# Short passages between the layers of a Fourier tokenizer, and in the block behind it: roots at the slots' end, keys in other banks, rows added in pairs on GpSimd

## The chip, the core and the metric

One NeuronCore of a Trainium2 chip runs the whole program. The metric is device microseconds of one execution. The engines are named as in the profile: PE is the matrix engine (TensorE), PEld its weight loads, DVE the VectorE, ACT the ScalarE, POOL the GpSimd and SP the engine whose queue issues the DMAs.

## The reference, cut to what matters

```
# tokenizer, 128 images of 64 x 64 x 3
h = layer_norm(x @ fc0_w + fc0_b)
for i in range(4):
    x1 = irfft2(einsum(rfft2(h)[12 x 12 modes, both corners], w1/w2[i]))   # the "mix" over modes
    x2 = einsum('bchw,oc->bohw', h, conv_w[i]) + conv_b[i]                 # 1x1 convolution
    h  = layer_norm(x1 + x2, ln_g[i], ln_b[i]);  h = gelu(h) if i < 3 else h
h = gelu(gelu(h @ fc1) @ fc2) @ fc3
h = concat(cls_tok, h)                       # 128 x 65 tokens of 64
# scan sublayer, on layernorm(h) = x and its flip xf
h_t = exp(delta A) h_(t-1) + delta Bf x + delta_b Bb xf;   y_t = sum over 16 states of C_n h_n
h = h + (y + x D_skip + xf D_skip) @ W_out.T
# attention and experts, on layernorm(h) = x
x = x + attention(rmsnorm(x));  out = sum over the top 2 of 8 experts of gate * (silu(f w1) * (f w3)) w2
h = h + x + out
```

## The kernel before, in words

**Tokenizer, to 5766 us.** A first pass goes over the 128 images two at a time, and stores each image's activations (1 MB for a pair, `act_scratch`) and its spectrum (`spectrum_in`). Then four layers follow. Each has a mix over the 12 vertical frequencies ky (`pe_mix`, `dve_mix`, `act_mix`: x_in of one ky is loaded and turned, multiplied by that ky's mixing matrix `w_mix`, and stored to `spectrum_out`), and a pass over all images (convolution product from `act_in`, L508, inverse transforms from `z_in`, L495, layer norm, gelu, and the forward transforms for the next layer). The mixing matrix of a ky is made from raw weights: load w_raw, DVE centres it (L1041, L1044), PE spreads it by four products (`pe_combine`, L978) and DVE copies four banks into `w_mix` (L1055).

A **passage** is what lies between such phases. Into the mix, the SP queue (`layer_body` and `sp_layer`) issues the two raw weights, the convolution's weight and bias, four pairs of gain and shift columns, the two rows of gain and shift, and only then x_in of the first two ky. DVE (`dve_layer`) waits for all of `layer_in` before it touches the convolution's weight and then the first raw weight. Out of the mix, `sp_load` issues act_in, z_in, act_in, z_in, and the first instruction of PE needs act_in.

**Block, from 5766.7 us.** 16 groups of 8 images (260 columns of tokens, 128 partitions) go through a software pipeline: in one window w, group w+1 is in its scan, group w in its attention, group w-1 in its experts. A window is a head and then 27 slots, whose order is written out in code for each engine by tables (`DRIVE_AT`, `SCAN_AT`, `READ_AT`, `OUT_AT`, `MEAN_AT`, ...): in slot n, PE does the three products of expert part n (`expert_slot`: w1 L1705, w3 L1710, w2 L1718) and a piece of the attention and the scan; DVE forms the gated hidden rows (L2165) and, a chunk of four states at a time, the scan's inputs (L2091, L2095, L2099), the scan (L2107) and the read product (L2113), whose rows PE multiplies by the output weights (L1741: four matmuls a chunk, one for each state). At the slots' end come the means and squares of three norms, at the next head their inverse roots: ACT guesses them by logs and exps (L1921, L1925), DVE does a Newton step (L2062, L2066, L2070), then xn, its flip xf, ue and un. PE waits there for xf (L1822). The head also holds the router's softmax and top 2 on DVE (L2184 to L2212), whose result PE turns (L1847) and casts to the expert rows (L1691), and the rotary products of queries and keys. The keys' two products (L1842, L1843) use the banks 5 and 6 that the queries' had, and so wait for DVE's L2080. GpSimd does four additions and products of 128 x 260 a window (L2295, L2298).

A dependency reads `wait(e, name, group, count)` in the code; ISA rows in an order listing are the semaphore instructions that stand apart from the work.

## Time and profile before

| | us |
|---|---|
| median of 3 runs | 7341.99 (7340.01 to 7343.35) |
| the profiled execution | 7339.24 |
| its span | 7337.5 |
| PE busy | 6634.3 (90%) |
| DVE busy | 4609.9 (63%) |
| ACT busy | 4417.8 (60%) |
| POOL busy | 3735.1 (51%) |

The program has two parts with different limits. The tokenizer lasts to 5766.7 us, with passages at 776.9, 1848.6, 2920 and 3993 us, where PE has nothing to do. The block lasts from there to the end. Its steady windows repeat every 92.16 us: `blk_bc`, the first work of ACT in a window, starts at 6008.8, and then twelve times every 92.16 us to 7114.8. A profile of the whole mixes them, so the rows below are of single stretches.

How to read it: a timeline row is start, duration, engine, line, operation, output and input, count, and in brackets the idle time of that engine just before it and what released it. Rows with a count join neighbours.

### The profile page before, as it was taken

How to read it: one execution, taken by the hardware profiler on the slowest of the kernel's cores; microseconds unless marked ns; L12 is line 12 of the kernel's file. 1: busy time of each engine (PE TensorE's matmuls, PEld its weight loads, DVE VectorE, ACT ScalarE, POOL GpSimd, SP SyncE). 2: the span in 40 equal slices, each digit the busy share in tenths (PEclk: the TensorE clock that was granted, in tenths of full speed). 3: DMA queues.
4: the chain of work that ended last, by engine and by line, in shares of the span. 5: the costliest groups of instructions: out<-in, count | busy, mean ns of one | idle time of the engine just before them, and what ended most of it. 6: DMA issues, size and time to landing. Idle time of an engine off the chain costs nothing. (4 is left out here: it accounts for less than half of the span.)

```text
span 7337.5 us, 138677 instructions
## 1 busy us (share of the span) xinstructions
PE 6634.3 (90%) x43890; PEld 4056.0 (55%) x43890; DVE 4609.9 (63%) x7185; ACT 4417.8 (60%) x8385; POOL 3735.1 (51%) x1348
## 2 busy tenths in 40 slices
PE   8999799999799998899998899999999578888888
PEld 3444566666566665666665544444444255555555
DVE  8999477777477776577776333333333477777774
ACT  5666466766466766466765577777777434444443
POOL 8999278777178776277775244444444100000000
PEclk9999899999899999999999999999999788888888
DMA  2333455554455554555554311111111333333330
GB/s 98 112 110 113 168 164 165 166 170 158 167 169 165 167 169 150 175 169 165 166 170 146 126 47 53 48 47 47 54 47 47 104 81 74 74 74 74 74 74 3
DMA packets 597030, 835.12 MB, mean 114 GB/s; under 512 B 451944, under 2 KB 493032, under 8 KB 531304
## 3 DMA queue, kind: packets, MB, share of 16 engines
q1 hardware_dynamic: 596968, 834.34, 36.6%
q8 instruction: 33, 0.54, 0.0%
q14 instruction: 29, 0.24, 0.0%
HBM read 477.60 MB, written 356.58 MB: 114 GB/s over the span
## 5 line engine op out<-in xcount | busy, mean ns | idle before, releaser
L949 POOL TENSOR_TENSOR sb_rstd<-sb_var,sb_minus_half 128x16 f32<-128x16 f32 x1280 | 3689.7, 2899 | 2047.8 <-DVE sb_var L900 1019.6
L691 DVE TENSOR_TENSOR sb_unit<-H,sb_rstd 128x512 f32<-128x512 f32 x768 | 529.1, 689 | 684.0 <-POOL sb_rstd L949 545.9
L508 PE MATMUL H<-sb_conv_block,sb_act_in 128*128 128x128 f32 x6144 | 825.3, 283 | 35.4 <-DMA sb_act_in<-act_scratch 28.7
L508 PEld LDWEIGHTS H<-sb_conv_block,sb_act_in 128*128 128x128 f32 x6144 | 731.6, 192 | 150.1 <-issue 140.9
L613 ACT ACTIVATE sb_act_px<-sb_unit 128x512 f32<-128x512 f32 x768 | 484.0, 630 | 499.5 <-DVE sb_unit L697 499.5
L2295 POOL TENSOR_TENSOR blk_pos<-blk_pos,blk_mag 128x260 f32<-128x260 f32 x32 | 22.8, 734 | 1337.3 <-ACT blk_mag L1961 1337.3
L636 ACT ACTIVATE sb_act_out<-TC 128x512 f32<-128x512 f32 x768 | 447.7, 583 | 180.8 <-PE TC L523 180.8
L912 DVE COPY sb_act_out<-TC 128x512 f32<-128x512 f32 x256 | 177.0, 691 | 595.3 <-PE TC L758 595.3
L775 PE MATMUL M<-sb_dense,sb_fc_w 128*64 128x512 f32 x2048 | 521.7, 609 | 30.4 <-ACT sb_dense L858 25.4
L697 DVE TENSOR_TENSOR sb_unit<-sb_unit,sb_shift_row 128x512 f32<-128x512 f32 x768 | 531.4, 692 | 26.1
L694 DVE TENSOR_TENSOR sb_unit<-sb_unit,sb_gain_row 128x512 f32<-128x512 f32 x768 | 531.2, 692 | 26.2
L684 DVE TENSOR_REDUCE sb_var<-sb_square 128x16 f32<-128x528 f32 x768 | 501.1, 694 | 69.7 <-ACT sb_square L606 69.7
L523 PE MATMUL TC<-sb_table,sb_act_px 128*128 128x128 f32 x3072 | 485.0, 281 | 62.5 <-ACT sb_act_out L636 62.1
L858 ACT ACTIVATE sb_dense<-M,sb_fc_shifted 128x512 f32<-128x512 f32 x512 | 323.8, 683 | 291.3 <-PE H L767 291.3
L537 PE MATMUL TP<-sb_act_px,sb_table 128*52 128x256 f32 x3072 | 496.5, 402 | 0.0
L523 PEld LDWEIGHTS TC<-sb_table,sb_act_px 128*128 128x128 f32 x3072 | 333.4, 142 | 256.0 <-ACT sb_act_px L613 218.6
L606 ACT ACTIVATE sb_square<-H 128x512 f32<-128x512 f32 x768 | 417.0, 600 | 94.7 <-PE H L516 94.7
L2009 ACT ACTIVATE blk_silu<-bank 114x260 f32<-114x260 f32 x384 | 148.6, 387 | 524.0 <-PE bank L1710 523.8
L516 PE MATMUL H<-sb_v_sb,sb_table 52*128 52x512 f32 x1536 | 433.7, 641 | 0.0
L495 PEld LDWEIGHTS M<-sb_table,sb_z_in 96*52 96x52 f32 x6144 | 357.5, 128 | 113.3 <-issue 81.8
L495 PE MATMUL M<-sb_table,sb_z_in 96*52 96x128 f32 x6144 | 404.6, 274 | 0.0
L864 ACT ACTIVATE sb_dense<-M,sb_fc_bias 128x512 f32<-128x512 f32 x512 | 352.0, 688 | 85.0 <-PE M L775 60.2
(274 smaller groups left out, 12749.6 us busy)
## 6 DMA issues: line engine op xcount, KB each, us to landing
act_scratch<-sb_act_out SPq DMA_DIRECT2D x256, 1024.0 KB, 3.9
sb_act_in<-act_scratch SPq DMA_DIRECT2D x256, 1024.0 KB, 5.3
spectrum_in<-sb_f_sb SPq DMA_DIRECT2D x512, 78.0 KB, 1.8
sb_x_in<-spectrum_in SPq DMA_DIRECT2D x48, 832.0 KB, 4.4
spectrum_out<-sb_y_sb SPq DMA_DIRECT2D x48, 832.0 KB, 4.6
sb_z_in<-spectrum_out SPq DMA_DIRECT2D x512, 78.0 KB, 5.1
blk_rows_b<-scan_rows SPq DMA_DIRECT2D x128, 260.0 KB, 6.6
blk_rows_bb<-scan_rows SPq DMA_DIRECT2D x128, 260.0 KB, 7.5
```

Of the source, the lines that this page charges most:

```text
L495: mm = e.matmul(M[u][64 * t:64 * t + 52, 128 * g:128 * g + 128], z, gb[:, t], start=True, stop=True, skip_group_check=True)
L508: e.matmul(H[j][:, 128 * u:128 * u + 128], act_in[p][:, 128 * b:128 * b + 128], conv_block[:, :], start=(u == 0), stop=False, skip_group_c ...
L523: mm = e.transpose(TC[:, 128 * u:128 * u + 128], act_px[k % 2][:, 128 * u:128 * u + 128], const("ident"))
L537: mm = e.matmul(dst, const("f1"), src[:, :, 16 * h:16 * h + 16], start=True, stop=True, skip_group_check=True)
L613: e.activation(act_px[k % 2][:, :], unit[k % 2][:, :], gelu).then_inc(px_ready, 1)
L636: e.activation(act_out[q][:, 512 * k:512 * k + 512], TC[:, :], ACT.Copy).then_inc(act_ready, 1)
L684: e.tensor_reduce(var[j][:, :], square[j % 2][:, :].rearrange("p (y c) -> p y c", c=C + 1), AX.X, ALU.add).then_inc(var_ready, 1)
L691: e.tensor_tensor(rows, H[k][:, :].rearrange("p (y c) -> p y c", c=C), rstd[k][:, :].unsqueeze(2).to_broadcast([128, 16, C]), ALU.mult).th ...
L694: e.tensor_tensor(rows, rows, gain_row[:, :].unsqueeze(1).to_broadcast([128, 16, C]), ALU.mult).then_inc(scaled, 1)
L697: e.tensor_tensor(rows, rows, shift_row[:, :].unsqueeze(1).to_broadcast([128, 16, C]), ALU.add).then_inc(affine_ready, 1)
L775: mm = e.matmul(FC1[w][64 * v:64 * v + 64, :], fc2_w[:, :], dense1[2 * w + v][:, :], start=True, stop=True, skip_group_check=True)
L949: e.tensor_tensor(rstd[j][:, :], var[j][:, :], minus_half[:, :], ALU.pow).then_inc(rstd_ready, 1)
```

## The change

Tokenizer. The gain and shift columns, which the last layer alone reads, are loaded once at the start. The convolution's weight and bias and the first two raw weights of a layer are loaded during the phase before (`sp_conv`), with a semaphore of their own (`conv_in`). In the passage SP issues x_in first, then the two rows, then both act_in (`sp_load_act`), which before were issued after the mix. DVE centres ky 0 and PE does its convolution product and first combine in banks of H, ahead of the waits for the last activations and spectra. After the mix, only z_in is left to load. At the start, the queue has four more DMAs ahead of the first image.

Block. The guesses, the table load and the Newton steps of the scan's and the experts' norm move from the next head to the slots' end. The keys' products go to banks 1 and 2, and wait for `bc` and `soft_pos` (ACT's reads of these banks) instead of `rope` 2. The first cast of the gate moves behind the first w1 product. GpSimd adds xn and xf into xs, so that the skip takes one product instead of two, and for each chunk adds the second half of its rows to the first (128 x 520), so that the output takes two matmuls instead of four.

The SP queue from the end of the first pass. In the listing `sb_` tiles are the tokenizer's, and act_scratch, spectrum_in and spectrum_out are in HBM. Before:

```order
L1190 DMA sb_w_raw<-in_w_mix_dram 128x416
L1192 ISA
L1062 ISA
L1062 DMA sb_conv_raw<-in_conv_w_dram 32x32
L1063 ISA
L1063 DMA sb_bias_raw<-in_conv_b_dram 32x1
L1068 REGISTER_ALU
L1072 DMA sb_gain<-in_ln_g_dram 32x1
L1073 DMA sb_shift<-in_ln_b_dram 32x1
```

and after:

```order
L1216 ISA
L972 DMA sb_x_in<-spectrum_in 128x1664 x2
L1205 REGISTER_ALU
L1075 ISA
L1075 DMA sb_gain_row<-in_ln_g_dram 128x32
L1076 DMA sb_shift_row<-in_ln_b_dram 128x32
L1208 REGISTER_ALU
L234 ISA
L258 DMA sb_act_in<-act_scratch 128x2048 x2
L1192 UNCONDITIONAL_BRANCH
L1192 ISA
L970 ISA
```

The loads of x_in have moved ahead of all, and the two of act_in stand where the mix's own loads of w_raw (L970) come next.

PE at the head of a window, from the keys' products (`blk_wk_rot`) to the second slot. `blk_lg` holds the gate, `blk_gate_t` the gate turned, `blk_ue` and `blk_ug` are the experts' inputs. Before:

```order
L1843 MATMUL bank<-blk_un,blk_wk_rot 128x260
L1569 ISA
L1847 MATMUL bank<-blk_tables,blk_lg 16x65 x4
L1691 MATMUL bank<-blk_gate_t,blk_pick 128x260
L1569 ISA
L1700 MATMUL bank<-blk_res,blk_tables 128x260
L1705 MATMUL bank<-blk_ue,blk_experts 114x260
L1569 ISA
L1710 MATMUL bank<-blk_ug,blk_experts 114x260
```

and after:

```order
L1862 MATMUL bank<-blk_un,blk_wk_rot 128x260
L1582 ISA
L1866 MATMUL bank<-blk_tables,blk_lg 16x65 x4
L1713 MATMUL bank<-blk_res,blk_tables 128x260
L1718 MATMUL bank<-blk_ue,blk_experts 114x260
L1704 MATMUL bank<-blk_gate_t,blk_pick 128x260
L1582 ISA x2
L1727 MATMUL bank<-blk_ug,blk_experts 114x260
```

The cast (`blk_pick`) has moved behind the residual's product and the first w1 product.

ACT at the slots' end, where `blk_sn` is the scan's norm, `blk_mn` the experts' and `blk_an`, `blk_un` the attention's. Before:

```order
L2011 ACT_TABLE_LOAD
L1569 REGISTER_ALU
L1886 ACTIVATE blk_sn_sqr<-bank 128x260
L1887 ACTIVATE blk_h_cen<-bank 128x260
L1892 ACTIVATE blk_mn_sqr<-blk_x 128x260
L1903 ACTIVATE blk_h<-bank 128x260
L1897 ACTIVATE blk_an_sqr<-bank 128x260
L1898 ACTIVATE blk_cen<-bank 128x260
L1609 REGISTER_ALU
L1609 COMPARE_AND_BRANCH
L1921 ACTIVATE blk_sn_log<-bank,blk_tables 128x260
```

and after:

```order
L1904 ACTIVATE blk_sn_sqr<-bank 128x260
L1905 ACTIVATE blk_h_cen<-bank 128x260
L1582 REGISTER_ALU
L2031 ACTIVATE blk_silu<-bank 114x260
L1910 ACTIVATE blk_mn_sqr<-blk_x 128x260
L2046 ACT_TABLE_LOAD
L1921 ACTIVATE blk_h<-bank 128x260
L1932 ACTIVATE blk_sn_log<-bank,blk_tables 128x260
L1932 ACTIVATE blk_mn_log<-bank,blk_tables 128x260
L1582 ISA
L1936 ACTIVATE blk_sn_y<-blk_sn_log 128x260
```

The scan's squares now stand ahead of the last silu, and the two logs ahead of the loop's branch, with the attention's squares behind them.

The diff, cut to its core (in its second half PE's code comes first, then ACT's `guesses`, DVE's `roots` behind the slots, and GpSimd's additions):

```diff
         def sp_load_act(e, P, p, n):
             at_least(e, h_ready, 8 * P + 4 * p - 4)
             e.dma_start(act_in[p][:, :], act_d[n]).then_inc(ld[p], 16)
...
         def pe_combine(e, m, p, layer):
+            banks = H if isinstance(m, int) and q == 0 else COMBINED
...
         def pe_mix(e, m, p, layer, more):
+            if zero:
+                e.wait_ge(w_mix_s, 4 * q0 + 4)
             turn(0)
...
+        def sp_rows(e, norm):
+            g, b = norm
             e.dma_start(gain_row[:, :], g.partition_broadcast(128)).then_inc(layer_in, 16)
             e.dma_start(shift_row[:, :], b.partition_broadcast(128)).then_inc(layer_in, 16)
+        def sp_conv(e, layer):
+            e.dma_start(conv_raw[:, :], io["conv_w"][layer]).then_inc(conv_in, 16)
+            e.dma_start(bias_raw[:, :], io["conv_b"][layer].unsqueeze(1)).then_inc(conv_in, 16)
+            for p in range(2):
+                e.dma_start(w_raw[p][:, :], io["w_mix"][layer, p]).then_inc(w_in[p], 16)
...
             def layer_body(layer, last):
                 for p in range(2):
-                    e.dma_start(w_raw[p][:, :], io["w_mix"][layer, p]).then_inc(w_in[p], 16)
+                    e.wait_ge(st_x[p], 32 * halves * (layer + 1))
+                for p in range(2):
+                    sp_mix_load(e, 0, p, layer)
                 e.wait_ge(act_ready, 8 * halves * (layer + 1))
-                sp_layer(e, layer + 1, layer, (io["ln_g"][layer], io["ln_b"][layer]))
+                sp_rows(e, (io["ln_g"][layer], io["ln_b"][layer]))
+                for p in range(2):
+                    e.wait_ge(st_a[p], 16 * halves * (layer + 1))
+                    sp_load_act(e, halves * (layer + 1), p, p)
                 mix(layer)
...
-        WO_AT, X2_AT, H1_AT = 22, 23, 25
+        WO_AT, X2_AT, H1_AT = 22, 23, 24
-        SKIP_AT = 9
+        SKIP_AT = 12
-        MEAN_AT, VARIANCE_AT = 23, 24
+        MEAN_AT, VARIANCE_AT = 22, 24
...
                     e.matmul(B[0][0:2 * HP, 0:TOK], expert("w1", x, k, 2 * HP), ue[:, :], start=True, stop=True)
+                    if n == 0:
+                        gate_cast(g, 0)
                     if k == 0:
                         wait(e, "ug", g, x + 1)
+                    if n < 2 and attn is not None:
+                        wait(e, "rope", attn, 5 + n)
...
-                    e.matmul(B[7][:, 0:TOK], wskip[:, :], xn[:, :], start=True, stop=False, skip_group_check=True)
-                    e.matmul(B[7][:, 0:TOK], wskip[:, :], xf[:, :], start=False, stop=False, skip_group_check=True)
+                    wait(e, "both", g)
+                    e.matmul(B[7][:, 0:TOK], wskip[:, :], xs[:, :], start=True, stop=False, skip_group_check=True)
...
-                    wait(e, "read", g, k + 1)
-                    for n in range(NC):
-                        mm = e.matmul(B[7][:, 0:TOK], wt("wout"), wide(rows_c, k)[:, TOK * n:TOK * n + TOK],
+                    wait(e, "paired", g, k + 1)
+                    for half in range(2):
+                        mm = e.matmul(B[7][:, 0:TOK], wt("wout"), wide(rows_c, k)[:, TOK * half:TOK * half + TOK],
...
-                    wait(e, "rope", ga, 2)
-                    e.matmul(B[5][:, 0:TOK], wt("wk_t"), un[:, :], start=True, stop=True)
-                    e.matmul(B[6][:, 0:TOK], wk_rot[:, :], un[:, :], start=True, stop=True).then_inc(sig["qk"], 1)
+                    if scan:
+                        wait(e, "bc", gs)
+                        wait(e, "soft_pos", gs)
+                    e.matmul(B[1][:, 0:TOK], wt("wk_t"), un[:, :], start=True, stop=True)
+                    e.matmul(B[2][:, 0:TOK], wk_rot[:, :], un[:, :], start=True, stop=True).then_inc(sig["qk"], 1)
...
+                    if n == VARIANCE_AT:
+                        guesses(w + 1, scan1, moe1)
...
+                roots(w + 1, scan1, moe1)
...
+                    e.tensor_tensor(xs[:, :], xn[:, :], xf[:, :], ALU.add).then_inc(sig["both"], 1)
+                if scan:
+                    for k in range(CHUNKS):
+                        wait(e, "read", gs, k + 1)
+                        rows = wide(rows_c, k)
+                        e.tensor_tensor(rows[:, 0:2 * TOK], rows[:, 0:2 * TOK], rows[:, 2 * TOK:4 * TOK],
+                                        ALU.add).then_inc(sig["paired"], 1)
```

## Rows read from the trace of the kernel before

**Rows 1.** Windows: stretch, its length, busy us (x instructions), PEclk, DMA share, GB/s

```profile
776.90:788.30 11.40, 0.00 (x0) 0.00 (x0) 0.00 (x1) 0.00 (x0) 0.00 (x0) 0.50 0.34 83
895.20:904.60 9.40, 0.00 (x0) 0.00 (x0) 0.00 (x0) 0.41 (x2) 0.00 (x0) 0.68 0.72 229
6009.00:7115.00 1106.00, 922.04 (x3843) 641.75 (x3842) 797.78 (x1392) 473.47 (x1105) 33.74 (x48) 0.87 0.32 74
```

**Rows 2.** Page, DMA issues: count, KB each, us to landing

```profile
sb_act_in<-act_scratch SPq DMA_DIRECT2D x256, 1024.0 KB, 5.3
sb_x_in<-spectrum_in SPq DMA_DIRECT2D x48, 832.0 KB, 4.4
sb_z_in<-spectrum_out SPq DMA_DIRECT2D x512, 78.0 KB, 5.1
```

**Rows 3.** Timeline of SP, first passage into the mix

```profile
776.87 0.78 SPq L264 DMA_DIRECT2D spectrum_in<-sb_f_sb  x2
...
785.21 0.90 SPq L963 DMA_DIRECT2D sb_x_in<-spectrum_in  x2
```

**Rows 4.** Timeline of DVE, first passage and the start of the mix

```profile
788.30 0.21 DVE L1079 COPY sb_conv_rep<-sb_conv_raw 32x128 f32<-32x128 f32 x1 [18.96 <-DMA sb_shift_row<-in_ln_b_dram]
...
797.44 0.56 DVE L1041 TENSOR_REDUCE sb_w_sum<-sb_w_raw 128x13 f32<-128x416 f32 x1
...
801.69 0.86 DVE L1055 COPY sb_w_mix<-TC 128x416 f32<-128x416 f32 x1 [3.06 <-PE TC L978]
```

**Rows 5.** Timeline of PE, start of the mix

```profile
796.51 1.08 PE L992 MATMUL H<-sb_table,sb_x_in 128*128 128x128 f32 x8
...
806.33 1.13 PE L1005 MATMUL H<-sb_w_mix,sb_x_t 128*128 128x128 f32 x8 [0.44 <-ACT sb_x_t L1023]
```

**Rows 6.** Timeline of SP, passage out of the mix

```profile
899.21 0.35 SPq L252 DMA_DIRECT2D sb_act_in<-act_scratch  x1
```

**Rows 7.** Timeline of PE, passage out of the mix

```profile
904.62 2.07 PE L508 MATMUL H<-sb_conv_block,sb_act_in 128*128 128x128 f32 x8 [9.54 <-DMA sb_act_in<-act_scratch]
906.62 3.01 PE L495 MATMUL M<-sb_table,sb_z_in 96*52 96x128 f32 x32
```

**Rows 8.** Timeline of PE, start of the program

```profile
18.82 0.64 PE L294 MATMUL M<-sb_table,sb_image_in 128*96 128x128 f32 x2 [7.53 <-DMA sb_image_in<-in_x_dram]
```

**Rows 9.** Timeline of PE, end of the window 6469.7 to 6561.9

```profile
6545.67 1.92 PE L1741 MATMUL bank<-blk_rows_c,blk_weights 128*128 128x260 f32 x8
...
6558.87 1.21 PE L1822 MATMUL bank<-blk_xn,blk_w_delta 128*128 128x260 f32 x2 [3.46 <-DVE blk_xf L2247]
```

**Rows 10.** Timeline of ACT, end of that window

```profile
6549.34 1.28 ACT L2011 ACT_TABLE_LOAD   x1
...
6554.47 0.48 ACT L1921 ACTIVATE blk_sn_log<-bank,blk_tables 128x260 f32<-128x260 f32 x1
```

**Rows 11.** Timeline of PE, head of that window

```profile
6476.89 1.23 PE L1842 MATMUL bank<-blk_un,blk_weights 128*128 128x260 f32 x2 [3.12 <-DVE blk_tmp L2080]
...
6479.95 0.60 PE L1847 MATMUL bank<-blk_tables,blk_lg 65*16 65x65 f32 x4 [0.96 <-DVE blk_lg L2212]
6481.95 1.23 PE L1691 MATMUL bank<-blk_gate_t,blk_pick 16*128 16x260 f32 x2 [1.40 <-ACT blk_gate_t L1984]
...
6485.01 1.08 PE L1710 MATMUL bank<-blk_ug,blk_experts 128*114 128x260 f32 x2
```

**Rows 12.** Timeline of DVE, that window

```profile
6474.78 0.66 DVE L2196 TENSOR_TENSOR blk_lg<-blk_lg,blk_tables 65x64 f32<-65x64 f32 x1
...
6477.97 0.22 DVE L2196 TENSOR_TENSOR blk_lg<-blk_lg,blk_tables 65x64 f32<-65x64 f32 x1
...
6520.68 1.23 DVE L2113 TENSOR_TENSOR blk_rows_c<-blk_rows_c,blk_rows_b 128x1040 f32<-128x1040 f32 x1
...
6542.77 0.43 DVE L2165 TENSOR_TENSOR blk_hid<-blk_silu,bank 114x260 f32<-114x260 f32 x1 [3.42 <-ACT blk_silu L2009]
```

**Rows 13.** Timeline of GpSimd, that window

```profile
6474.62 0.73 POOL L2298 TENSOR_TENSOR blk_dub<-blk_pos,blk_xf 128x260 f32<-128x260 f32 x1
```

More of the change, by code:

```diff
@@ L1050, in dve_mix @@
             q, q0 = 2 * m + p, NY * layer
+            banks = H if isinstance(m, int) and q == 0 else COMBINED
             since(e, y_pe, 4 * q0, 4 * (q - 1))
@@ L1938, in window, with before @@
                     guess(moe_n, "x")
+            def before(w, scan, attn, moe):
+                scan_square(w, scan)
+                guesses(w, scan, moe)
+            def window(w, scan, attn, moe, scan1, attn1, moe1):
+                gs, ga, gx = w + 1, w, w - 1
+                old = moe and not (isinstance(gx, int) and gx == 0)
                 if attn:
```

112 lines of the change are left out of this document (55 added, 57 removed).

## The prediction, as it was made before the changed kernel had run

> **What bounds the kernel now.** I read the windows view first, to find stretches in which PE has nothing to do, since the page has it at 90% of the span and nothing else near that. Then the timelines of SP, DVE and PE in one such stretch of each kind, then one steady window of the block on every engine.
>
> There are two kinds of stretch. The first are passages between the tokenizer's phases. Before a mix, PE, DVE and ACT all stand still for 11.4 us [rows 1], and the next row of DVE says for what: it sat 18.96 us until the row of shifts had landed [rows 4]. That load is the last of fourteen, most of them tiny, which SP issues between the last spectrum's store at 776.87 and x_in at 785.21 [rows 3]. PE's first turn of x_in comes at 796.51 [rows 5]. After a mix, PE waits 9.54 us for act_in, issued at 899.21, and takes up z_in at 906.62 [rows 6, 7]. All this happens four times.
>
> The second kind are waits inside the block's window. Over twelve windows in 1106 us (92.16 each) PE is busy 922.04, that is 76.8 of 92.2 us [rows 1]. The rest is in two places of a window. At its end PE waits 3.46 us for xf, the last link of squares, logs, roots [rows 9]. In its head it waits 3.12 for the queries' rotation, 0.96 for the gate and 1.40 for the turned gate [rows 11]. DVE is nearly full in the middle, and its first long idle time, 3.42 us, comes at 6542.77, where it waits for ACT behind PE [rows 12]. So from there to the end PE sets the pace, and in the middle both do.
>
> **The passages, part by part.** *Into the mix.* SP's gain and weight loads go out of the way. x_in can go when the stores from 776.87 are in, which I put at 779.4; before it went at 785.21 [rows 3], so it lands 5.8 earlier, and no longer waits for a turn behind the combine: with 4.4 us to land [rows 2] and 1.2 for what it shares with its twin, the first turn is near 785.0 instead of 796.51, 11.5 us earlier. The convolution, centring and combine of ky 0, which filled 788.3 to 796.5, now run before 777, under the last images' work of ACT and SP.
>
> That gain is not kept in full. What is late next is the raw weight of ky 2. It stands behind x_in (2 x 832 KB) and act_in (2 x 1024 KB), 3.7 MB, which at the 229 GB/s of the loads in the other passage [rows 1] take 16.2 us: it lands at 795.6 instead of before 797.44. DVE's centring of ky 2 comes ahead of its copies for ky 1 in its order, and takes 1.2; the copies then begin at 796.8 where they began at 801.69 [rows 4], and the mix of ky 1, which began 4.6 later at 806.33 [rows 5], is 4.9 us earlier. If the weight's packets pass beside the large loads, it is up to 9. I take 6 a layer. Bounds: 2 (x_in slowed by act_in from its own first packet) and 11.5.
>
> *Out of the mix.* act_in is in memory, and L508 (2.07 us) starts at once. z_in goes at 899.21 instead of 0.4 to 3 us behind it, and its landing no longer shares the rings with 2 MB. PE took z_in at 906.62; the second z load now goes at about 899.9, and with between 2 and 5.1 us to land [rows 2] PE takes it at 902 to 905. I take 902.3, so 4.3 less; bounds 1.5 and 4.9.
>
> *At the start* four more DMAs stand before the first image, and PE waits for the image [rows 8]. Fourteen took the 7.6 us between the first row's end and the last row of [rows 3], 0.54 each: +2.
>
> Tokenizer: 4 x (6 + 4.3) - 2 = 39 us less; with all bounds at one side 12 to 64.
>
> **The block, part by part, per window.** *Roots at the slots' end.* ACT's silu of the last part ends as its table load starts, at 6549.34, and the first log is at 6554.47 [rows 10], 5.13 later, because four squares and copies, two means and a third square stand between. Now the scan's squares are before the last silu, and between are one square, the load (1.28) and h, the two at 0.3 each: 1.9. From the log to L1822 the links are the same ones, 4.40 (6554.47 to 6558.87 [rows 9, 10]). So L1822 comes 3.2 us sooner after the last silu. Late next are the attention's squares, which stand behind the guesses. Their roots end at about 2.5 us after xf, and PE has three products and the router's (3.6 us) to do in that time, so this is covered; if not, it costs up to 1. Bounds 2.2 and 3.5.
>
> *Fewer products.* The output takes 8 instead of 16, the skip 1 instead of 2. An L1741 group of four is 1.92 as x8 rows, which is 0.44 for each product, so 9 x 0.44 = 4.0 of PE. It counts only where PE sets the pace: the last two groups (the fourth is that of 6545.67 [rows 9]) and the skip, 5 x 0.44 = 2.2. Bounds 1.3 and 4.0.
>
> *The gate's first cast.* PE waits 1.40 for the turned gate and then does L1691, L1700 and L1705, and w3 at 6485.01 [rows 11]. Now L1700 and L1705, 1.9 together at this clock, run in the wait, and w3 can come when the cast (6481.95 to 6483.1) and ug (0.4) are done, at 6483.8: 1.2 less. Bounds 0 and 1.3. The new wait of slots 0 and 1 for the keys' rotation is met by then: DVE does it right behind the gate's chain, while PE turns the gate.
>
> *The keys' banks.* The 3.12 us wait goes, but the gate's chain on DVE is not shortened by it, and L1847 stays at 6479.95 [rows 11]. The wait is moved, not removed: 0. A price is possible: PE, idle in one piece of 4.5 us instead of 3.1 and 1.0, is at its lower clock for longer. A pair of passes takes about 1.0 us at this clock, against 0.44 after it; four more such products would cost 2.2. Bounds 0 and +2.2.
>
> *GpSimd's additions.* One product of 128 x 260 took 0.73 [rows 13], so one of 128 x 520 is estimated at 1.46, and four and xs are 6.6 us a window. GpSimd has the time, but DVE does not run freely beside it: the same L2196 took 0.66 while GpSimd worked (6474.62 to 6475.35), and 0.22 without [rows 12, 13]. An addition starts when its read product ends, the first at 6521.9 [rows 12], and the fourth falls in DVE's idle time. Three times 1.46 are 4.4 us which DVE can lose, and it had 3.42 of idle time at 6542.77. But PE waits within the middle for hidden rows too, so the idle time at the end does not absorb it all. I take half, +2.2, and +0.2 for xs beside the gate's chain. Bounds 0 and +6.6.
>
> The Trainium skill, SBUF — State Buffer, section "Who interferes with whom", says that a VectorE instruction with two SBUF inputs and a GpSimd instruction that reads SBUF exclude one another for their whole length, whichever came first. The stretched L2196 agrees. By this rule the scan of 2.3 us can also hold back an addition, which would then come to PE 3.8 us after its read; by a rule of shared bandwidth neither would. It is a mechanism of the slower rival, below, and its price there is from the rows.
>
> Sum: -3.2 - 2.2 - 1.2 + 0 + 2.4 = -4.2 us a window. There are thirteen full windows (twelve of the row, and the one before them, of 91.7): -55. The windows that fill and drain the pipeline have the roots or the products, not both: -1 each for four, -4. Block: -59. Bounds with all at one side are -8.8 and +3.9 a window. I hold -7.5 to +0 as its likely part, -100 to 0.
>
> **Total.** 39 + 59 = 98 us less than the profiled execution's 7339.2, 7241. The median of the three runs is 2.8 above that execution, so 7244 as a median.
>
> **Rivals.**
>
> *Only the passages pay.* The additions take back from DVE what PE gains, and a window stays within 1 us of 92.16. For it speaks that DVE is full in the middle and loses up to 4.4; against it, that the roots' 3.2 us lie outside that stretch. Then 7342 - 39 = 7303.
>
> *The block pays in full.* The additions fall beside DVE's work with one input from PSUM, and all nine products count: -8 a window, 13 x 8 = 104. For it speaks that L2165 and L2161 read a bank; against it, that the scan, the three inputs and the read itself have both inputs in SBUF. Then 7342 - 39 - 104 = 7199.
>
> *x_in gains nothing*, because the two act_in share its rings, as they did with z_in, whose median of 5.1 for 78 KB is that of a megabyte. The passages then pay 2 + 4.3 a layer, less 2: 23, and the time is 7342 - 23 - 59 = 7260.
>
> *Slower.* The additions stand in the scan's way, or it in theirs: DVE loses all 6.6 us, and PE, in its order, waits for `paired` about 1 us at the two chunks where product follows read by 3 us (8.6). DVE's lag carries to the last silu, so the roots give nothing; products and cast give 3.4. A window is then 5.2 us longer, 13 windows 68, and 7342 - 39 + 68 = 7371. It decides from 39 / 13 = 3.0 us a window on.
>
> **How the numbers follow.** Forecast 0.50, only the passages 0.15, the block in full 0.18, x_in gains nothing 0.12, slower 0.05. The range for 8 in 10: from the full case, 7195, to the case of the passages alone, 7303. A measurement of this kernel can tell about 0.2%, 15 us, from no change. All cases but the last lie beyond it; some of the case of the passages alone lies within if both bounds are bad. Faster 0.92, same 0.03, slower 0.05.
>
> **What would show it.** In the profile after: DVE's wait for the shift row gone, the first turn about 8 us after the last spectrum store, and then DVE waiting for w_raw of ky 2 in a row of its own; if it does not wait, the passage gives near 11. PE's wait for act_in after the mix replaced by one of some 5 us for z_in. In a steady window, an interval near 88 us, L1822 some 6.7 us after the last silu; L1842 without a wait and L1847 with one of 4 to 5 us; L2107 or L2091 of 1.5 us more than 2.3 and 1.2 where an addition runs beside them; GpSimd's additions of 1.4 to 1.5 us. The forecast is wrong if the window is over 91 or under 85, or if the passages give under 5 us a layer in all.

## The result, and the profile after

| | before | changed |
|---|---|---|
| median us | 7340.75 (5 runs) | 7304.17 (7299.74 to 7311.40, 5 runs) |
| ratio, 95% interval | | 0.995 (0.9936 to 0.9965) |
| span of the profiled execution | 7337.5 | 7297.9 |
| first `blk_bc` of the block | 5784.4 | 5752.4 |
| from there to the end | 1553.0 | 1545.5 |
| mean of twelve steady windows | 92.17 | 91.61 |

Every median is of fast executions; one slow one of experiment 7 (10486.97 us at a granted clock of 0.555) is left out, with which its median would be the 7210 that the expectation of experiment 14 names.

The kernel became 36.6 us faster, where 98 were forecast, and its time is one microsecond above the range. Of the 39.5 us of the span, 32.0 come ahead of the block. The block was to give 59 and gave 7.5 in this execution; the first experiment below has it at nothing.

**The passages.** First SP at the first passage, as [rows 3]; columns as there.

```profile
778.88 0.79 SPq L273 DMA_DIRECT2D spectrum_in<-sb_f_sb  x2
781.23 0.84 SPq L972 DMA_DIRECT2D sb_x_in<-spectrum_in  x2
...
783.61 0.86 SPq L258 DMA_DIRECT2D sb_act_in<-act_scratch  x2
784.99 0.34 SPq L970 DMA_DIRECT2D sb_w_raw<-in_w_mix_dram  x1
```

x_in leaves 2.3 us behind the last store, not 8.3 [rows 3]. Then PE and DVE, which answer to [rows 4, 5]:

```profile
786.43 1.20 PE L1002 MATMUL H<-sb_table,sb_x_in 128*128 128x128 f32 x8 [0.95 <-DVE sb_w_mix L1068]
```

```profile
795.38 0.59 DVE L1053 TENSOR_REDUCE sb_w_sum<-sb_w_raw 128x13 f32<-128x416 f32 x1 [9.01 <-DMA sb_w_raw<-in_w_mix_dram]
796.00 0.59 DVE L1056 SCALAR_TENSOR_TENSOR sb_w_cen<-sb_w_sum,sb_w_raw 128x416 f32<-128x416 f32 x1
796.51 0.85 DVE L1068 COPY sb_w_mix<-TC 128x416 f32<-128x416 f32 x1
```

The first turn is at 786.43 instead of 796.51, and DVE waits 9.01 us for the raw weight of ky 2, up to 795.38 (the prediction had it land at 795.6). Its copies for ky 1 begin at 796.51, 5.2 us earlier than before. Behind the mix and at the start, as [rows 7, 8]:

```profile
901.19 3.66 PE L504 MATMUL M<-sb_table,sb_z_in 96*52 96x128 f32 x32 [6.35 <-DMA sb_z_in<-spectrum_out]
```

```profile
20.80 0.63 PE L303 MATMUL M<-sb_table,sb_image_in 128*96 128x128 f32 x2 [10.32 <-DMA sb_image_in<-in_x_dram]
```

z_in is taken up 5.4 us earlier, and the image 2.0 later. Of the 5.4 us, 2.1 come from ahead of this passage: the mix's last row of PE (L1005, now L1017) starts at 891.57 instead of 893.64. The passage out of the mix alone gives 3.4.

**The block.** The windows view over the twelve steady windows, as the last of [rows 1], and then three stretches of the head of the window from 6436.69 (columns: PE, PEld, DVE, ACT, POOL busy; PEclk, DMA share, GB/s):

```profile
5979.73:7079.09 1099.36, 898.71 (x3626) 602.38 (x3626) 823.22 (x1392) 472.47 (x1104) 158.60 (x108) 0.85 0.31 74
6436.69:6445.69 9.00, 3.67 (x27) 3.02 (x26) 6.04 (x20) 8.99 (x25) 3.50 (x5) 0.88 0.61 160
6445.69:6452.69 7.00, 4.96 (x13) 2.65 (x14) 2.83 (x10) 5.78 (x14) 0.00 (x0) 0.50 1.04 259
6452.69:6458.69 6.00, 6.00 (x16) 3.33 (x16) 2.04 (x5) 1.04 (x3) 0.00 (x0) 0.62 1.04 255
```

and the same three of before (window from 6469.69):

```profile
6469.69:6478.69 9.00, 5.88 (x27) 4.64 (x26) 6.05 (x20) 8.58 (x23) 2.81 (x4) 0.69 0.66 157
6478.69:6485.69 7.00, 4.65 (x13) 2.58 (x12) 2.65 (x10) 6.21 (x14) 0.00 (x0) 0.50 1.05 244
6485.69:6491.69 6.00, 5.92 (x22) 3.38 (x22) 3.23 (x7) 1.35 (x4) 0.00 (x0) 0.96 1.05 232
```

Before, the granted clock was 0.69 in the first nine microseconds and back at 0.96 from 16 us on. Now it is 0.88 in the first nine, where PE mostly waits, and 0.62 from 16 to 22 us, where it works without a pause: 16 instructions in 6 us instead of 22. GpSimd's rows at the end of the middle, then PE and DVE beside them:

```profile
6398.53 6.25 POOL L2337 TENSOR_TENSOR blk_rows_c<-blk_rows_c 128x520 f32<-128x520 f32 x1 [47.20 <-DVE blk_rows_c L2139]
6407.78 1.28 POOL L2337 TENSOR_TENSOR blk_rows_c<-blk_rows_c 128x520 f32<-128x520 f32 x1 [3.00 <-DVE blk_rows_c L2139]
6413.19 1.29 POOL L2337 TENSOR_TENSOR blk_rows_c<-blk_rows_c 128x520 f32<-128x520 f32 x1 [4.13 <-DVE blk_rows_c L2139]
```

```profile
6404.84 1.14 PE L1758 MATMUL bank<-blk_rows_c,blk_weights 128*128 128x260 f32 x4 [1.94 <-POOL blk_rows_c L2337]
6405.82 0.42 PE L1782 MATMUL bank<-blk_tables,blk_sc 65*65 65x65 f32 x4
6406.05 1.13 PE L1718 MATMUL bank<-blk_ue,blk_experts 128*114 128x260 f32 x2
```

```profile
6398.71 2.32 DVE L2133 TENSOR_TENSOR_SCAN blk_rows_b<-blk_dA,blk_rows_b 128x1040 f32<-128x1040 f32 x1
6400.94 0.40 DVE L2191 TENSOR_TENSOR blk_hid<-blk_silu,bank 114x260 f32<-114x260 f32 x1
6401.26 1.23 DVE L2117 TENSOR_TENSOR blk_rows_b<-blk_rows_b,blk_du 128x1040 f32<-128x1040 f32 x1
6402.41 1.23 DVE L2121 TENSOR_TENSOR blk_rows_bb<-blk_rows_bb,blk_dub 128x1040 f32<-128x1040 f32 x1
6403.75 2.13 DVE L2125 TENSOR_TENSOR blk_rows_b<-blk_rows_b,blk_rows_bb 128x1040 f32<-128x1040 f32 x1
```

The first addition of a window lasts 6.25 us and the others 1.28. While it lasts, DVE does a scan and two inputs at their usual length, and only the third input is stretched, from 1.24 to 2.13. So, by my estimate from these rows (the addition's end less its usual 1.28), GpSimd came to its work at about 6403.5 and was shut out for 5 us before. Over the block's 16 windows this addition lasts 6.25 us eleven times, 3.95 three times, and 5.58 and 3.23 once each in the filling windows. Where it lasts 3.95, as here, DVE's first input (L2117) is the stretched one, 2.32 instead of 1.23:

```profile
6491.38 3.95 POOL L2337 TENSOR_TENSOR blk_rows_c<-blk_rows_c 128x520 f32<-128x520 f32 x1 [48.33 <-DVE blk_rows_c L2139]
```

So it got in two of DVE's inputs sooner there. What decides this the rows do not show. PE waits for the addition, and the next pair of passes, of L1718, takes 1.13 instead of 0.60.

At the slots' end, ACT and PE, as [rows 9, 10]:

```profile
6427.76 1.28 ACT L2046 ACT_TABLE_LOAD   x1
...
6429.34 0.47 ACT L1932 ACTIVATE blk_sn_log<-bank,blk_tables 128x260 f32<-128x260 f32 x1
```

```profile
6433.72 1.20 PE L1839 MATMUL bank<-blk_xn,blk_w_delta 128*128 128x260 f32 x2 [1.56 <-DVE blk_xf L2272]
```

From the last silu (6427.05) to this product are 6.67 us, and were 9.93 (6548.94 to 6558.87): 3.26 less. In the head, as [rows 11]:

```profile
6355.42 0.60 PE L1866 MATMUL bank<-blk_tables,blk_lg 65*16 65x65 f32 x4 [6.58 <-DVE blk_lg L2238]
6355.81 1.18 PE L1713 MATMUL bank<-blk_res,blk_tables 128*128 128x260 f32 x2
```

The same, as means over twelve windows, in us after the window's `blk_bc`. Silu n is ACT's silu of slot n, and "gate turned" is the start of PE's turn of it (L1847, now L1866); the last four columns are experiments 3, 5, 7 and 2 of the next section.

```
                     before  changed  late adds  filler   both   without adds
gate turned           10.3    10.4     10.4      10.5    10.5    10.4
silu 0                16.4    15.9     15.9      14.8    14.6    15.9
silu 3                21.8    23.2     23.3      19.7    21.0    23.5
silu 13               49.4    50.0     50.9      46.5    48.5    50.8
first output product  55.3    60.3     57.8      56.7    54.8    57.9
silu 17               60.7    66.7     63.3      63.3    60.3    63.5
silu 23               79.3    82.7     79.3      79.2    76.3    82.1
delta product         89.2    89.3     85.9      85.9    82.9    88.7
next window           92.2    91.6     88.8      88.4    84.8    91.2
```

Read down the second column against the first: 0.5 ahead at silu 0, 1.4 behind at silu 3 (the clock), 5 behind at the first output product, 3.4 behind at silu 23 (six products saved since), level at the delta product (the roots).

### The profile page after: what moved, and what is told of

It is laid out like the page before. It is cut to its first block and busy times, and to the rows that moved or that the text cites. A ratio compares the mean times of both kernels' runs of the same rounds, so it can differ in the third digit from the quotient of the medians.

```text
span 7297.9 us, 138227 instructions
## 1 busy us (share of the span) xinstructions
PE 6617.4 (91%) x43602; PEld 4015.1 (55%) x43602; DVE 4644.3 (64%) x7185; ACT 4417.2 (61%) x8385; POOL 3905.2 (54%) x1428
## 3 DMA queue, kind: packets, MB, share of 16 engines
q1 hardware_dynamic: 595432, 834.33, 36.6%
## 5 line engine op out<-in xcount | busy, mean ns | idle before, releaser
L2337 POOL TENSOR_TENSOR blk_rows_c<-blk_rows_c 128x520 f32<-128x520 f32 x64 | 158.8, 2481 | 907.9 <-DVE blk_rows_c L2139 907.9
```

## The experiments

The theory after this reading: the passages work as forecast. The block's gains are real, but two things take them back: the chunk 0 addition, which DVE shuts out, and the stretch at PE's lower clock, which has moved out of the head into slots 0 to 2. The rivals: it is the clock alone, it is DVE slowed by every addition, or one of the other edits costs.

**1. The tokenizer part alone.** The changed kernel's code up to the block, and the block of before.

> The tokenizer part of the change alone, the block as before. By the profile of the changed kernel the block starts 32.0 us sooner (its first blk_bc at 5752.4 against 5784.4) and the block itself gives 7.5. If the two parts are independent, this kernel is 32 us under before, 7309. Rival: the block gains part of its 7.5 from the passages or loses by them; then this kernel is 25 or 40 under before.

Measured: 7304.37 (7299.84 to 7305.43), ratio 0.995 (0.9936 to 0.9964), as the changed kernel. So the passages give 36.7 and, by the medians, the block's edits together nothing. Its block starts at 5744.9, 39.6 us earlier, and its windows are 92.16 again. The start of the block scatters by 8 us between executions with this same tokenizer (5744.9 to 5753.5 in the profiles of the first five kernels that have it): why was not looked into. A difference of under 8 us between two kernels can therefore be the tokenizer's.

**2. Without the additions.**

```diff
-                    wait(e, "paired", g, k + 1)
-                    for half in range(2):
+                    wait(e, "read", g, k + 1)
+                    for n in range(NC):
...
```

and GpSimd's loop over the chunks is left out.

> The changed kernel without GpSimd's additions of the rows: the output takes four matmuls a chunk again, straight behind the read products. Theory (additions): the first addition of a window, shut out by DVE, holds PE up at the first output product and costs more than all the saved products give; the window (91.6 us mean in the changed kernel) becomes 88 to 90, and the run 7262 to 7285. Rival (clock): the loss stands in the slots' first third, where PE is at its lower clock after a longer idle time; then the window gets longer by the eight products, 8 x 0.44 = 3.5, to 95, and the run is about 7345.

Measured: 7290.53, ratio 0.9926 (0.9912 to 0.9939). It is 13.6 us faster than the changed kernel with eight products more in each window. Against experiment 1 the rest of the block's edits give 14 us, where the forecast without additions and their products would be -3.2 - 1.2 - 0.4 a window, 62 us. So the additions explain a part, and something else takes 48 us more.

**3. The addition of chunk 0 left out.**

```diff
-                    wait(e, "paired", g, k + 1)
-                    for half in range(2):
+                    by = k >= 1
+                    wait(e, "paired" if by else "read", g, k + 1 - (1 if by else 0))
+                    for n in range(2 if by else NC):
...
-                    for k in range(CHUNKS):
+                    for k in range(1, CHUNKS):
```

> The changed kernel with GpSimd's additions for chunks 1 to 3 only; chunk 0 is read by four matmuls as before. In the changed kernel the additions of chunks 1 to 3 last 1.28 us each and only that of chunk 0 lasts 4 to 6.3 us. Theory (the starved first addition): the window loses the 4 to 5 us of the first output product and keeps 6 of 8 saved products: 87 to 89, the run 7250 to 7270. Theory (every addition costs DVE its length): the window falls only by a quarter of the loss, to about 90.5, the run 7290. Rival (clock): no change but the two products more, 92.5 and 7316.

Measured: 7257.59, ratio 0.9884 (0.9869 to 0.99): 46.6 us less than the changed kernel, with two products more. Against experiment 2 it has six products fewer a window, which at 0.44 are 13 x 2.6 = 34 us, and it is 33 faster. So the late additions cost nothing that shows, although in the changed kernel the scan behind them took 2.40 and 2.62 instead of 2.32, and the whole price is that of chunk 0's.

**4. Chunk 0's addition alone.** The same with `by = k == 0` and `range(1)`.

> The changed kernel with GpSimd's addition for chunk 0 alone; chunks 1 to 3 are read by four matmuls. Theory (the addition that DVE shuts out): it lasts 4 to 6.3 us as in the changed kernel, L1758 for chunk 0 waits for it, and the kernel is the changed one plus 6 x 0.44 us a window: 94.2, 7304 + 34 = 7338. If it is not chunk 0's place but the sum of four additions that starves the first, it lasts 1.3 here and the kernel is under that without additions (7290.5) by 0.9 us a window: 7279.

Measured: 7353.84, ratio 1.002 (1.0011 to 1.0029), 63 us more than without additions. With the two products that it saves a window (13 x 0.9 = 11) the addition costs 75 us, 5.7 a window. Both stated numbers were too low. The mechanism holds: the addition lasts 6.02 us in the mean of all 16 windows, with no other addition near it. GpSimd's group of these additions over the block (count, busy us, mean ns, idle time before):

```profile
L2338 POOL TENSOR_TENSOR blk_rows_c<-blk_rows_c 128x520 f32<-128x520 f32 x16 | 96.3, 6018 | 732.1 <-DVE blk_rows_c L2140 732.1
```

and that of experiment 3:

```profile
L2338 POOL TENSOR_TENSOR blk_rows_c<-blk_rows_c 128x520 f32<-128x520 f32 x48 | 69.6, 1450 | 970.0 <-DVE blk_rows_c L2140 970.0
```

Here eleven windows in a row are 95.54 to 95.57 long, and silu 3 stands at 23.2 in them.

**5. Unused matmuls in the wait for the gate.** Nobody reads their product; they only keep PE at work.

```diff
+                if moe and attn and scan:
+                    wait(e, "soft_mag", gs)
+                    for q in range(12):
+                        e.matmul(B[0][:, 0:TOK], wt("wq_t"), un[:, :], start=True, stop=True)
                 if moe:
                     wait(e, "gate", gx)
```

> The changed kernel with twelve matmuls more in each full window, whose product is not used (un by the query weights into bank 0, overwritten by the first w1), in the stretch where PE waits 6.6 us for the gate: 12 x 0.44 = 5.3 us. They change no other engine's work. Theory (clock): PE comes into slot 0 at its full clock, and L1713, L1718, L1704, L1727 to the third slot take 0.44 instead of 0.9 to 1.0 a product, 2 us a window less, 89.6 and 7278. If the longer idle time does not matter: 91.6 and 7304 as the changed kernel, or more if the twelve delay the gate's turn.

Measured: 7258.98, ratio 0.9892 (0.9877 to 0.9907): 45.2 us less than the changed kernel, by more work. Silu 3 is 3.5 us earlier in the window, twice what was expected. Its stretches of the head, for the window from 6413.56:

```profile
6413.56:6422.56 9.00, 9.00 (x47) 7.96 (x47) 6.04 (x20) 8.60 (x23) 3.51 (x5) 0.84 0.63 165
6422.56:6429.56 7.00, 5.39 (x24) 2.99 (x23) 3.73 (x13) 6.46 (x15) 0.00 (x0) 1.00 1.05 244
6429.56:6435.56 6.00, 5.92 (x24) 3.56 (x23) 4.17 (x7) 1.16 (x3) 0.00 (x0) 1.00 1.03 238
```

In the last two of these stretches the granted clock is 1.00 (the upper level, 2.4 GHz), where it was 0.50 (the lower level, 1.2 GHz) and 0.62. The low clock is not gone: in this window it now lies 45 to 70 us behind `blk_bc`, beside the first addition and behind it,

```profile
6458.56:6471.56 13.00, 9.17 (x32) 5.07 (x31) 12.79 (x14) 2.32 (x6) 6.25 (x1) 0.72 0.03 6
6471.56:6483.56 12.00, 12.00 (x63) 8.71 (x62) 9.87 (x12) 4.07 (x11) 2.57 (x2) 0.88 0.00 0
```

where the changed kernel had 0.87 and 1.00. So the 45 us are what the move of the low stretch gives, and not the whole price of the low clock.

**6. The same without additions.**

> The changed kernel without additions of rows, with the twelve unused matmuls in the wait for the gate. If they act by the clock alone, they give what they gave beside the additions, 45 to 48 us of 7290.5: about 7244. If they acted by letting the first addition in sooner, they give under 15 here.

Measured: 7229.63, ratio 0.9849 (0.9832 to 0.9865), 61 us less than experiment 2. So the unused matmuls act without any addition. The profiled execution is the slowest of the five (7274.49; the fastest took 7223.96), and it shows two kinds of window one after the other: four of 85 us, one of 86.6, and from there on only those of 92.1. From each kind two stretches, 45 to 58 and 58 to 70 us after `blk_bc`:

```profile
6181.94:6194.94 13.00, 13.00 (x65) 9.29 (x64) 12.79 (x15) 4.23 (x11) 0.00 (x0) 0.87 0.03 6
6194.94:6206.94 12.00, 12.00 (x64) 8.77 (x63) 9.25 (x11) 3.47 (x9) 0.00 (x0) 1.00 0.00 0
...
6814.42:6827.42 13.00, 9.85 (x34) 6.12 (x33) 12.79 (x16) 2.31 (x6) 0.00 (x0) 0.72 0.03 7
6827.42:6839.42 12.00, 12.00 (x59) 8.70 (x59) 8.07 (x8) 3.47 (x9) 0.00 (x0) 0.87 0.00 0
```

In the long kind the low clock lies over slots 13 to 17, where PE has no time to spare. Eight of the profiled windows are of the long kind, so the faster executions probably have fewer of them; they have no trace.

**7. Both: experiments 3 and 5 together.**

> Both edits that helped, together: GpSimd's additions for chunks 1 to 3 only, and the twelve unused matmuls in the wait for the gate. Alone they gave 47 and 45 us against the changed kernel. Theory (two places): the one removes the late first output product, the other the slow clock in slots 0 to 2, so they add: about -90, 7212. Rival (one place): both only bring DVE's and PE's work in slots 13 to 17 into a better order, and together they give little more than either, 7250.

Measured: 7206.55, ratio 0.9819 (0.9806 to 0.9831). That is 98 less than the changed kernel, and 46.6 and 45.2 make 92: they are two places.

**8. Unused matmuls in slot 12 as well.**

```diff
                     wait(e, "both", g)
+                    if attn is not None:
+                        for q in range(5):
+                            e.matmul(B[7][:, 0:TOK], wskip[:, :], xs[:, :], start=True, stop=True, skip_group_check=True)
```

> As combo, and five unused matmuls more in slot 12 ahead of the skip product (xs by the skip weights into bank 7, overwritten by it), where PE waits 2.44 us for the silu behind the softmax's exps and then ran at 1.07 us a pair of passes instead of 0.60. If the clock is the cause there too, slots 12 to 15 take 1 to 2 us less a window, 7195 or less. If DVE, which has no idle time there, sets the pace, as combo, or 5 x 0.44 us more where the wait was shorter than they are.

Measured: 7262.10, ratio 0.9891 (0.9877 to 0.9905), 56 us more than without them. Silu 13 comes 1.8 us sooner (46.7 against 48.5), and silu 17 3.6 later. PE has closed the gap in slot 12, and then stands in slot 14, where it waits for DVE, and behind that the clock is low (0.61 from 55 to 65 us into the window, where experiment 7 has 1.00):

```profile
6467.14 0.69 PE L1727 MATMUL bank<-blk_ug,blk_experts 128*114 128x260 f32 x2 [2.82 <-DVE blk_hid L2199]
...
6469.50 1.21 PE L1718 MATMUL bank<-blk_ue,blk_experts 128*114 128x260 f32 x2
...
6473.70 3.67 PE L1762 MATMUL bank<-blk_rows_c,blk_weights 128*128 128x260 f32 x8
```

The eight passes take 3.67, and at the upper clock 1.92 [rows 9]. So filling this gap did not pay, because another followed it ahead of work in which PE sets the pace. Neither stated case was this one.

**9. The keys' products in the queries' banks, on experiment 3.** The wait for `rope` 5 and 6 in slots 0 and 1 is out as well.

```diff
-                    if scan:
-                        wait(e, "bc", gs)
-                        wait(e, "soft_pos", gs)
-                    e.matmul(B[1][:, 0:TOK], wt("wk_t"), un[:, :], start=True, stop=True)
+                    wait(e, "rope", ga, 2)
+                    e.matmul(B[5][:, 0:TOK], wt("wk_t"), un[:, :], start=True, stop=True)
...
```

> As the kernel with additions for chunks 1 to 3 only (7257.6), but the keys' products in the queries' banks again, behind the wait for the queries' rotation. PE's idle time in the head is then 3.1 and about 1 us in two pieces instead of 6.6 in one. Theory (clock): the move to other banks costs, for PE comes colder into slot 0: without it a window is 1 to 2 us shorter, 7232 to 7245. The prediction's value for this move was 0: then 7258.

Measured: 7259.69, ratio 0.9887 (0.9873 to 0.9902), 2 us from 7257.59: the forecast's 0 holds, the clock theory's form of this one fails. Silu 3 is at 23.2 as without the edit.

**10. The gate's first cast in the head, on experiment 3.**

```diff
                     mm.then_inc(sig["gate_turned"], 1)
+                    gate_cast(gx, 0)
...
-                    if n == 0:
-                        gate_cast(g, 0)
```

> As the kernel with additions for chunks 1 to 3 only (7257.6), with the first gate cast in the head again, ahead of L1700 and L1705 of the kernel before. Forecast for this step: -1.2 us a window, so without it 7257.6 + 13 x 1.2 = 7273. From the profile, where the first silu came 0.55 sooner in the window: 7265. If the place does not decide, 7258.

Measured: 7250.76, ratio 0.9878 (0.9863 to 0.9893), 7 us faster without the move, against a forecast of 16 slower. That is within the scatter of the block's start (experiment 1). In the two profiles the steady windows are alike, most of them 88.63 to 88.68 us with the move and without it; what differs is the last window (85.02 against 88.77) and the 217 or 222 us behind it. So the move gives nothing in a steady window, and it is not shown to cost anything.

**11. The roots in the next head, on experiment 3.** The square of the experts' norm and the table load are where they were before, too.

```diff
-        WO_AT, X2_AT, H1_AT = 22, 23, 24
-        MEAN_AT, VARIANCE_AT = 22, 24
+        WO_AT, X2_AT, H1_AT = 22, 23, 25
+        MEAN_AT, VARIANCE_AT = 23, 24
...
-                    if n == VARIANCE_AT:
-                        guesses(w + 1, scan1, moe1)
+                guesses(w, scan, moe)
...
-                roots(w + 1, scan1, moe1)
+                roots(w, scan, moe)
```

> As the kernel with additions for chunks 1 to 3 only (7257.6), with the roots back in the next head: guesses behind the attention's squares, DVE's Newton steps at the window's start, tables 23, 24, 25 as before. The step was forecast at -3.2 us a window, and the profile shows 6.68 us from the last silu to the first delta product against 9.93. Theory (the gain is real, and paid for in part by PE's lower clock, which without the longer wait falls in the first slots and not in the head's projections): the window grows by 3.25, by 0.7 in the head, and loses 2 in slots 0 to 2: 1.9 longer, about 25 us, 7283. If there is no such payment: 3.25 x 13 = 42 longer, 7300.

Measured: 7345.40, ratio 1.0002 (0.9993 to 1.0011), 88 us slower. From silu 23 to the next window are 13.6 us instead of 9.5, and silu 23 itself is 2.4 later, with first output products that scatter from 57.7 to 61.1. So the roots are worth more than forecast, 4.1 us at their place, and the payment in the head that I had assumed does not exist: silu 0 and silu 3 stand at 15.9 and 23.4 as with the roots moved. The windows of this kernel mostly last 93.4, 95.3 to 95.7 or 97.6 us. From 58 to 64 us into one of 97.6 the granted clock is 0.51, into one of 93.4 it is 1.00, as in experiment 3. So the other 2.4 us go with the place of the low clock.

**12. Both head edits undone, without and with additions.** Experiments 9 and 10 together, on 2 and on 3.

> The changed kernel without additions of rows, with the keys' banks and the cast as before: of the block's edits the roots, xs and the skip's slot are left. Theory (the roots' move brings the low clock into the slots, since the head no longer has it behind the 3.5 us wait): the first silu at 16.4 and the fourth over 23 us after blk_bc, window about 91, 7290 as without additions. Rival (the head's order did it): the fourth silu at 21.8 as before, window 92.2 - 3.3 - 0.4 = 88.5, 7256.

> The same with GpSimd's additions for chunks 1 to 3. Theory (roots): the fourth silu over 23 us, about 7250 to 7258, as with one of the two undone. Rival (the head's order): the fourth silu at 21.8, a window 1.5 to 2 us shorter, 7230.

Measured: 7277.38, ratio 0.9915 (0.9899 to 0.9932), and 7250.94, ratio 0.988 (0.9863 to 0.9896). In both, silu 3 stays over 23 us in the mean, so undoing the head's edits does not bring the low stretch back to its old place; nor does undoing the roots (experiment 11). The profile of the first shows what the place is worth, in two neighbouring windows of the same code. The three head stretches of each, then the lengths 87.56 and 93.16:

```profile
6600.70:6609.70 9.00, 5.70 (x27) 4.66 (x26) 6.04 (x20) 8.57 (x23) 3.50 (x5) 0.69 0.64 156
6609.70:6616.70 7.00, 4.82 (x14) 2.58 (x12) 2.83 (x10) 6.23 (x14) 0.00 (x0) 0.50 1.05 248
6616.70:6622.70 6.00, 5.92 (x22) 3.36 (x22) 3.21 (x7) 1.32 (x4) 0.00 (x0) 0.96 1.04 236
...
6688.26:6697.26 9.00, 4.50 (x27) 3.36 (x25) 6.86 (x23) 9.00 (x25) 3.50 (x5) 0.92 0.62 157
6697.26:6704.26 7.00, 5.32 (x14) 2.80 (x14) 2.83 (x10) 5.78 (x14) 0.00 (x0) 0.50 1.05 243
6704.26:6710.26 6.00, 6.00 (x16) 3.52 (x16) 2.04 (x5) 0.78 (x3) 0.00 (x0) 0.57 1.04 237
```

The first has the clock's pattern of before (0.69, 0.50, 0.96) and is 87.56 long: the forecast for these edits was 88.5. The second has that of the changed kernel, and is 5.6 longer. The kernel before kept to one pattern, twelve windows of 92.16 with a low stretch in the head. Others keep to one too, with the low stretch over slots 0 to 2 (experiment 4) or over slots 13 to 17 (the long kind of experiment 6), and in this kernel it changes from window to window.

**13. The raw weights of ky 2 and 3 ahead of act_in, on experiment 3.**

```diff
+        def sp_mix_raw(e, p, layer):
+            e.wait_ge(w_cen_s, NY * layer + p + 1)
+            e.dma_start(w_raw[p][:, :], io["w_mix"][layer, 2 + p]).then_inc(w_in[p], 16)
...
                 for p in range(2):
                     sp_mix_load(e, 0, p, layer)
+                for p in range(2):
+                    sp_mix_raw(e, p, layer)
                 e.wait_ge(act_ready, 8 * halves * (layer + 1))
```

> As the kernel with additions for chunks 1 to 3 only (7257.6), but the raw weights of ky 2 and 3 are issued straight behind x_in of ky 0 and 1, ahead of both act_in. In the changed kernel the weight of ky 2 was issued at 784.99 and landed at 795.35, and DVE waited 9.01 us for it. If it was the 2 MB of act_in ahead of it, it now lands before 790, the mix of each layer begins its second ky 4 to 5 us sooner, and the run is 12 to 20 us less, 7238 to 7246. If the load is then late elsewhere (x_in of ky 2 behind act_in), the gain is under 5.

Measured: 7248.61, ratio 0.9871 (0.9857 to 0.9886), 9 us less: between the two cases. DVE's wait shrank from 9.01 to

```profile
787.81 0.59 DVE L1057 TENSOR_REDUCE sb_w_sum<-sb_w_raw 128x13 f32<-128x416 f32 x1 [1.27 <-DMA sb_w_raw<-in_w_mix_dram]
```

and from the last spectrum's store to the first product of z_in each layer is 2.2 to 4.5 us shorter than in experiment 3.

**14. The best version: 3, 5 and 13 together; and it with the cast as in 10.**

> All that helped: additions for chunks 1 to 3 only, the twelve unused matmuls in the wait for the gate, and the raw weights of ky 2 and 3 ahead of act_in. The first two together gave 7210 and the third alone 9 us. They touch different phases, so they add: 7201, range 7193 to 7210.

> The best version so far (7199) with the first gate cast ahead of the residual and the first w1 again. Undone alone the cast gave 7 us (7250.8 against 7257.6). If PE's order there costs as such: 7192. In this kernel PE is at its full clock when it comes to the cast, so that the cast's move should do what it was forecast for, 0.5 to 1.2 us a window: then 7206 to 7215.

Measured: 7199.27, ratio 0.9805 (0.9792 to 0.9818), and 7204.44, ratio 0.9816 (0.9799 to 0.9832), which is no difference from it. The first is 140 us under before, and 105 under the changed kernel.

## Why the prediction was wrong, step by step

**Into the mix: right in the mean.** Forecast 6 a layer, after 11.5 less what the raw weight gives back. In the first layer the turn came 10.1 us earlier with everything before it 2.0 later, and the copies for ky 1 at 796.5 against a forecast of 796.8. By the end of the mix less of this was left. From the last spectrum's store to the last product of the mix, the four layers are 4.1, 8.5, 8.6 and 7.1 us shorter in the changed kernel's profile, 7.1 in the mean. Experiment 13 shows that act_in's place in the queue was a cause of the part given back.

**Out of the mix: within its bounds, over-sized.** From there to the first product of z_in it is 3.4, 3.7, 3.7 and 1.0 us less, 2.9 in the mean, where 4.3 were forecast with 1.5 as the lower bound.

**Start: right**, 2.0. **A term was missing:** the passes behind the first three mixes take 1.4 to 2.6 us longer each, 6 in all, for a reason that I did not look into.

The tokenizer's sum was 39. This profile has 28.4 + 11.6 - 6.0 - 2.0 = 32.0, and experiment 1 has 36.7 by its median.

**Roots: right in the chain, under-sized as a step.** 9.93 to 6.67 is 3.26, against 3.2. Undone, it costs 4.1 at this place, and 88 / 13 = 6.8 a window in all, the rest of it in the slots, with the clock's place (experiment 11).

**Fewer products: right at 0.44 each, under-counted.** Experiments 2 and 3 differ by six products a window, and all six count, not only those after DVE's idle time. The skip's one product for two, and the xs that it needs, were in every kernel with the block's edits and have no run of their own.

**Gate's cast: wrong.** -1.2 a window forecast; the steady windows are as long without the move in experiment 10, and the time is the same in 14.

**Keys' banks: 0, right** (experiment 9).

**PE's lower clock: the other step that failed.** Its bound, +2.2, is near what came in the head: from silu 0 to silu 3 are 7.3 us instead of 5.4. But the keys' move is not the reason, since they are as far apart without it. The wait for the gate became 6.58 us, where 4 to 5 were forecast: PE was busy for 3.67 of the first nine us at a clock of 0.88, and before for 5.88 at 0.69. I set the price of the lower clock at nothing. Experiment 2 fell 48 us short of its edits' forecast, and the twelve unused matmuls gave back 45, 61 and 51 us (experiments 5, 6 and 7), 3.5 to 4.7 a window. What I missed is that one change in a window moves the low stretch over other work. Experiments 9, 11 and 12 undo the head's edits or the roots, and in none of them does it go back for good. Where it lies is worth 5.6 us between two windows of one code (experiment 12).

**GpSimd's additions: the step that failed.** I priced them as a loss for DVE, three times 1.46, half of it. DVE lost 0.1 to 1.1 at each, and the later additions took 1.28. The loss is on GpSimd's side: in eleven of 16 windows the first addition waits through a scan and two inputs of DVE, each with two inputs in SBUF, and the first output product waits for it. By experiment 3 that is 46.6 us with two products given back: (46.6 + 13 x 0.9) / 13 = 4.5 us a window, and by experiment 4 it is 5.7, where the term was +2.2. The sentence on the Trainium skill's rule, SBUF — State Buffer, "Who interferes with whom", that the scan could hold an addition back, had the mechanism, and I put it into the slower rival at 5% with a delay of one instruction. The trace agrees with the rule that one fully blocks: DVE's scan and first two inputs keep their length, 2.32 and 1.23, beside an addition that lasts 6.25. It adds two things. The blocked addition mostly did not get in between DVE's instructions, although a product with one input in PSUM (L2191, 0.40) stood among them. And by the record, which is rough for GpSimd, the addition began 0.18 us ahead of the scan and was still the one that waited.

One sum of the prediction is wrong: with all bounds at one side the slow end of a window is -2.2 - 1.3 + 2.2 + 6.6 = +5.3, not +3.9. The stated range does not hang on it.

Of the rivals, "only the passages pay" (7303) is what happened, to a microsecond in number. Its reason, DVE's lost time, is not the one found: the block came to nothing because the first addition and the clock took back what roots and products gave, which is luck for the number.

What stays open: what decides at which window the low stretch moves. Experiment 6 has both patterns in one execution, and no run tells what switches them. The parts, measured one at a time on different kernels, do not add up to the block's nothing exactly, since each change moves the low stretch too. Nor was it tried to let GpSimd add chunk 0 in a later slot.

## What to carry to other kernels

When a kernel repeats to the hundredth of a microsecond, as this one did at 92.16, look where the low clock lies in its window, and price a change both with the low stretch there and with it over the work that sets the pace. Work handed to GpSimd beside a busy DVE can cost latency, here 6.25 us for 1.28, while DVE hardly slows: ask how soon its consumer needs it, and what DVE runs at that moment. And when a load is moved ahead, list what small loads now stand behind it: here 2 MB went ahead of 208 KB that DVE needed, and DVE waited 9.01 us.

## What the runs showed of the hardware that was not expected

- GpSimd's addition of 128 x 520 takes 1.28 us, less than twice the 0.73 of 128 x 260 [rows 13], and 3.95 to 6.25 us in the full windows where it meets DVE's scan and inputs.
- Twelve matmuls whose product nobody reads made the kernel 45 us faster (experiment 5), and five more in another gap cost 56 us (experiment 8).
- One code gives windows of 85 and of 92 us in one execution (experiment 6), and of 87.56 and 93.16 next to each other (experiment 12).
